# Attention with unnormalised probabilities: plain transposes, and the row sums divided out of the mixed rows

## The chip, the cores and the metric
One Trainium2 chip; the kernel runs on one of its cores. The metric is device time in microseconds (us), from the first to the last instruction and what lies around them. A measurement of this kernel can tell about 0.2% from no change.

## What is computed
An audio tower: patches become 8 x 376 tokens of 256 features; then attention, a mixture of experts, a linear recurrence and a quantised feed-forward layer, each added to its input. The change is in the attention, cut here to what matters:

```python
HEADS, DIM_HEAD = 16, 64
q = apply_rope(split_heads(x @ Wq)); k = apply_rope(split_heads(x @ Wk)); v = split_heads(x @ Wv)
sim = jnp.einsum('bid,bjd->bij', q, k) * d ** (-0.5)
sim = jnp.where(causal[None], sim, -jnp.inf)
attn = jax.nn.softmax(sim, axis=-1)
out = jnp.einsum('bij,bjd->bid', attn, v)      # batch 8, 376 tokens
return out @ Wo + bo
```

## The kernel before, in words
**Tiles.** A batch is 376 tokens in three tiles of 128, 128 and 120 rows (`TILES`, `TILE_ROWS`). The 16 heads go in 8 pairs c, as two heads of 64 features fill 128 partitions. Matrix products are made of float32r operands split into a high and a low part, three products each. Every engine has an instruction order written out by hand in `attention`, and semaphores tie the orders together. Each engine's queue is in order.

**A pair on TensorE** (`step`, L750). `turn` (L655) of the even head, `project` (L610) of q for the pair three ahead (`LEAD`), `scores` (L631) of the next pair, `turn` of the odd head, `mix` (L669) of the even head, `project` of k, `mix` of the odd head. `turn` brings the probabilities into the layout that `mix` needs: for each of the six causal blocks a matmul in f32 with a probability block as weights and a diagonal matrix of 1/row sum as the moving operand. So it transposes and normalises at once. It writes banks 4 and 5 (`BANK_PT`), columns 0 to 375. `mix` accumulates both heads of the pair in bank 6 (`BANK_O`), the even head in one half of the partitions, the odd one in the other.

**The same pair on ScalarE** (`step`, L884): `turned_high` (L841, the high part out of PSUM) of the even head, `raw_copy` (L819) of a projection, `exps` (L830) of the next pair's even head for the tile of 120 rows, `turned_high` of the odd head, the other five tiles' `exps`, `qk_split` (L824), `raw_copy`, `out_high` (L847, high part of the mixed rows), `qk_split`. In some steps `keep_turned` and `scale_rows` of the routing come in between.

**On VectorE** (`step`, L1155): `turned_low` (L1010, the low part), `swap_pairs` (L986, for the rotary embedding), `maxima` (L991) of the next pair, `turned_low` of the odd head, then `diagonals` (L1000) for both heads of the next pair: a reciprocal of the three row sums and a product of the identity with them; `swap_pairs`, and `out_low` (L1015). The maxima stand before the exponentials, since they are the bias.

**GpSimd** does the rotary products (L959, L961, L963) and the low part of q and k (L936), and scatters rows to the experts (L948).

**Between batches** (`begin`, L782): TensorE makes the values of tile 2 (L693), then the output projection of the last batch (L704, `output`), which waits for `out_low` of its last pair, then the other values.

Of the kernel before, what the change touches and what calls it, by code (L numbers as in the profile page):

```python
# [24 lines left out]
P = 128  # L25
BATCH = 8
TIME, FREQ = 750, 128
PATCH = 16
TOK = -(-TIME // PATCH) * (FREQ // PATCH)
# [3 lines left out]
HEADS, HEAD = 16, 64  # L33
# [4 lines left out]
TILES = -(-TOK // P)  # L38
TILE_ROWS = [min(P, TOK - P * i) for i in range(TILES)]
# [396 lines left out]
def attention(nc, psum, h0_rows, x_dram, weights, a, consts, ident, x_slots, h_rows, onehot, where, shared, raw_w, w_in,  # L436
              scattered, tables, made):

    ctx, sb, sem = scopes(nc, made)
    with ctx:  # L440
# [10 lines left out]
        cos = shared[:, 4 * TOK:5 * TOK]  # L451
        neg_max = sb("neg_max", [P, 2, 4])
        row_sum = sb("row_sum", [P, 2, 4])
        inv_sum = sb("inv_sum", [P, 2, 4])
        PROBS_AT = [0, P, 3 * P]
        probs = shared[:, 5 * TOK:SHARED_COLS].rearrange("p (u n) -> p u n", u=2)
        diag = sb("diag", [P, 2, TILES, P])
        pt = [sb(f"pt_{part}", [P, 2, 2, TOK], F32R) for part in ("high", "low")]
        o = [sb(f"o_{part}", [P, PAIRS, TOK], F32R) for part in ("high", "low")]
        resid = sb("resid", [P, T, DIM])  # L460
        h = sb("attn_h", [P, T, DIM])
# [33 lines left out]
        x_loaded = [sem(f"attn_x_loaded{u}") for u in range(2)]  # L495
        (resid_in, cleared, v_made, v_high, v_low, proj_made,
         raw_made, swap_made, rope_made, rot_made, qk_high, qk_ready, scores_made, max_made, exp_made,
         inv_made, diag_made, turned, pt_high, pt_ready, mixed, o_high, o_ready, out_made, out_kept) = (
            sem(n) for n in
            "resid_in cleared v_made v_high v_low proj_made "  # L500
            "raw_made swap_made rope_made rot_made qk_high qk_ready scores_made max_made exp_made "
            "inv_made diag_made turned pt_high pt_ready mixed o_high o_ready out_made out_kept".split())


        CR_RAW, CR_ROT, CR_SCORES, CR_EXP, CR_TURN, CR_PT, CR_MIX, CR_O, CR_QK = 1, 2, 4, 1, 2, 1, 2, 1, 2
# [23 lines left out]
        def probs_t(j):  # L529

            return (0, 0, TOK) if j == 0 else (1, 0, TOK - P) if j == 1 else (1, TOK - P, TOK - 2 * P)

        def padded(part, t, half):

# [26 lines left out]
        with nc.Block(no_gpsimd_drain=True) as block:  # L561
# [32 lines left out]
            def _(pe):  # L594
# [59 lines left out]

                def turn(b, h):  # L655

                    pe.wait_ge(diag_made, 16 * b + h + 1)
                    pe.wait_ge(pt_ready, 16 * b + h + CR_PT)
                    for j in range(TILES):
                        bank, col, _ = probs_t(j)  # L660
                        for it in range(j, TILES):
                            ni, nj = TILE_ROWS[it], TILE_ROWS[j]
                            at, src = col + P * (it - j), PROBS_AT[it] + P * j
                            last = pe.matmul(psum[0:nj, BANK_PT + bank, at:at + ni],  # L664
                                             probs[0:ni, h % 2, src:src + nj],
                                             diag[0:ni, h % 2, it, 0:ni], start=True, stop=True)
                    last.then_inc(turned, 1)

                def mix(b, h):  # L669

                    c, par = h // 2, h % 2
                    pe.wait_ge(pt_ready, 16 * b + h + 1 + CR_PT)
                    if par == 0:
                        pe.wait_ge(o_ready, 8 * b + c + CR_O)
                        if c == 0 and b:
                            pe.wait_ge(out_kept, T * b)
                    for j in range(TILES):
                        bank, col, n = probs_t(j)
                        nj = TILE_ROWS[j]
                        for i, (hv, hp) in enumerate(three):  # L680
                            last = pe.matmul(psum[:, BANK_O, P * j:TOK],
                                             v[hv][0:nj, j, c, HEAD * par:HEAD * par + P],
                                             pt[hp][0:nj, par, bank, col:col + n],
                                             start=(par == i == j == 0),
                                             stop=(par == 1 and i == 2 and j == TILES - 1))
                    last.then_inc(mixed, 1)

                def values(b, tiles):
                    for t in tiles:
                        for half in range(2):  # L690
                            for i, (hw, hx) in enumerate(three):
                                for c in range(2):
                                    last = pe.matmul(psum[0:TILE_ROWS[t], 2 * t + half, :],  # L693
                                                     x[:, b % 2, hx, c, P * t:P * t + TILE_ROWS[t]],
                                                     wv[hw][:, c, BANK * half:BANK * (half + 1)],
                                                     start=(i == c == 0), stop=(i == 2 and c == 1))
                            last.then_inc(v_made, 1)
# [12 lines left out]
                def turn_rows(b, c):  # L710

                    pe.wait_ge(x_made, T * (b + 1))
                    for k in range(T):
                        n = TILE_ROWS[k]
                        last = pe.transpose(turned_bank(b, c)[:, P * k:P * k + n], rows[0:n, b % 2, k, P * c:P * (c + 1)],
                                            ident[0:n, 0:n])
                    last.then_inc(x_turned, 1)
# [62 lines left out]
                def begin(b):  # L780

                    pe.wait_ge(pt_ready, 16 * b + CR_PT)  # L782
                    values(b, (2,))
                    if b:
                        pe.wait_ge(o_ready, 8 * b + CR_O)
                        output(b - 1, 0)
                        pe.wait_ge(raw_made, 16 * b + 2 * LEAD + CR_RAW)
                        output(b - 1, 1)
                        pe.wait_ge(out_kept, T * (b - 1) + 1)
                        output(b - 1, 2)  # L790
                    if b >= 2:
                        pe.wait_ge(out_kept, T * (b - 1) + 2)
                        ahead_of(b - 2)
                    pe.wait_ge(exp_made, 16 * b + 2 + CR_EXP)
                    values(b, (0, 1))
                    pe.wait_ge(v_low, 6 * b + 2)
# [9 lines left out]
                for t in range(T):  # L806
                    output(LAST, t, range(PAIRS - 1, PAIRS))
                pe.wait_ge(pt_ready, 16 * BATCH + CR_PT)
                turn_rows(LAST, 0)
                turn_rows(LAST, 1)  # L810
                logit(LAST)
# [3 lines left out]
            def _(act):  # L815
# [29 lines left out]
                                   ACT.Copy).then_inc(pt_high, 1)  # L845

                def out_high(b, c):  # L847
                    act.wait_ge(mixed, 16 * b + 2 * c + 2 + CR_MIX)
                    act.activation(o[0][:, c, :], psum[:, BANK_O, 0:TOK], ACT.Copy).then_inc(o_high, 1)

                def deviation(b):
# [124 lines left out]
            def _(dve):  # L976
# [20 lines left out]
                        if it != 0:  # L997
                            last.then_inc(max_made, 1)

                def diagonals(b, h):  # L1000

                    dve.wait_ge(exp_made, 16 * b + h + 1 + CR_EXP)
                    dve.reciprocal(inv_sum[:, h % 2, 0:TILES], row_sum[:, h % 2, 0:TILES]).then_inc(inv_made, 1)
                    dve.wait_ge(inv_made, 16 * b + h + 1)
                    dve.tensor_tensor(diag[:, h % 2, :, :],  # L1005
                                      ident[:].rearrange("p (o n) -> p o n", o=1).broadcast_to((P, TILES, P)),
                                      inv_sum[:, h % 2, 0:TILES].rearrange("p (t o) -> p t o", o=1)
                                      .broadcast_to((P, TILES, P)), ALU.mult).then_inc(diag_made, 1)

                def turned_low(b, h):  # L1010
                    dve.wait_ge(pt_high, 16 * b + h + 1)
# [143 lines left out]
                def step(b, c, more):  # L1155
                    ahead = 2 * (c + LEAD)
                    projects = more or ahead < 2 * PAIRS
                    turned_low(b, 2 * c)
                    if projects:
                        swap_pairs(b, ahead)  # L1160
                    if c + 1 < PAIRS:
                        maxima(b, c + 1)
                    elif more:
                        maxima(b + 1, 0)
                    if b and c == ROUTE_LOGITS:
                        weigh(b - 1)
                    turned_low(b, 2 * c + 1)
                    if b == LAST and c == ROUTE_PREFIX:
                        place_rows(b - 1)
                    if more or c + 1 < PAIRS:  # L1170
                        diagonals(b, 2 * c + 2)
                        diagonals(b, 2 * c + 3)
                    if projects:
                        swap_pairs(b, ahead + 1)
                    out_low(b, c)
                    if b == LAST and c == ROUTE_LOGITS + 1:
                        choose(b - 1)
                    if b == LAST and c == ROUTE_LOGITS - 1:
                        add_bo(b)
# [1 line left out]
                for n in range(2 * LEAD):  # L1181
                    swap_pairs(0, n)
                maxima(0, 0)
                diagonals(0, 0)
                diagonals(0, 1)
                for b in range(BATCH):
                    begin(b)
                    for c in range(PAIRS):
# [1152 lines left out]
```

## Time and profile before

| | us |
|---|---|
| three runs | 1788.4, 1790.22, 1790.29 (median 1790.22) |
| profiled execution | 1788.28 |
| its span, first to last instruction | 1786.5 |
| TensorE matmuls busy | 1525.2 (85% of the span) |
| VectorE busy | 1250.3 (70%) |
| ScalarE busy | 995.8 (56%) |
| GpSimd busy | 1019.2 (57%) |
| attention, 118 to 862 us: TensorE, VectorE, ScalarE, GpSimd busy | 723.0, 544.6, 473.2, 549.6 |

The profile names PE (TensorE matmul), PEld (its weight loads), DVE (VectorE), ACT (ScalarE), POOL (GpSimd). Durations of matmuls overlap, so their cost is read from the distance between starts. In each other queue too, an instruction can start a little before the one ahead of it has ended. L12 is line 12 of the kernel; tiles are named by the program's names (`expert_raw` is memory shared by the attention's raw, swapped and probability tiles). "[0.22 <-PE psum L664]" behind a row is idle time of the engine before it, and what ended it.

### The profile page before, as it was taken

How to read it: one execution, taken by the hardware profiler on the slowest of the kernel's cores; microseconds unless marked ns; L12 is line 12 of the kernel's file. 1: busy time of each engine (PE TensorE's matmuls, PEld its weight loads, DVE VectorE, ACT ScalarE, POOL GpSimd, SP SyncE). 2: the span in 40 equal slices, each digit the busy share in tenths (PEclk: the TensorE clock that was granted, in tenths of full speed). 3: DMA queues.
4: the chain of work that ended last, by engine and by line, in shares of the span. 5: the costliest groups of instructions: out<-in, count | busy, mean ns of one | idle time of the engine just before them, and what ended most of it. 6: DMA issues, size and time to landing. Idle time of an engine off the chain costs nothing. (4 is left out here: it accounts for less than half of the span.)

```text
span 1786.5 us, 31373 instructions
## 1 busy us (share of the span) xinstructions
PE 1525.2 (85%) x11301; PEld 1440.1 (81%) x11301; DVE 1250.3 (70%) x2526; ACT 995.8 (56%) x2138; POOL 1019.2 (57%) x814
## 2 busy tenths in 40 slices
PE   5389999999999999999499999999998937689129
PEld 4279999999999998998399999999987836688029
DVE  6547676868677877776346766666678569559896
ACT  4547575657575757665355555455544434459552
POOL 4479586969687777864466767766765633000000
PEclk8679999999999999999699999999999968899569
DMA  6490000000001001000465555555554331003313
GB/s 237 147 300 19 18 19 25 31 25 30 25 14 38 13 22 33 4 31 10 154 177 143 144 136 146 135 147 140 140 136 107 71 96 35 18 1 130 104 52 113
DMA packets 86129, 150.44 MB, mean 84 GB/s; under 512 B 7992, under 2 KB 63608, under 8 KB 85720
## 3 DMA queue, kind: packets, MB, share of 16 engines
q1 hardware_dynamic: 75464, 134.62, 24.6%
q0 software_dynamic: 10512, 13.83, 4.6%
q8 instruction: 90, 1.47, 0.4%
q14 instruction: 63, 0.52, 0.1%
HBM read 111.88 MB, written 49.91 MB: 91 GB/s over the span
## 5 line engine op out<-in xcount | busy, mean ns | idle before, releaser
L1534 POOL TENSOR_TENSOR expert_w_low<-expert_raw,expert_w_high 128x768 fp32r<-128x768 f32 x152 | 288.3, 1946 | 170.3 <-ACT expert_w_high L1359 164.3
L835 ACT ACTIVATE expert_raw<-psum,neg_max 120x376 f32<-120x376 f32 (+2 forms) x384 | 176.0, 479 | 99.3 <-DVE neg_max L996 99.2
L664 PE MATMUL psum<-diag,expert_raw 128*128 128x128 f32 (+2 forms) x1536 | 198.9, 279 | 8.2 <-DVE diag L1005 7.3
L1012 DVE TENSOR_TENSOR pt_low<-psum,pt_high 128x752 fp32r<-128x752 f32 x128 | 120.5, 941 | 118.1 <-ACT pt_high L844 118.1
L1506 DVE TENSOR_TENSOR expert_act_low<-expert_act,expert_act_high 128x384 fp32r<-128x384 f32 x152 | 140.1, 921 | 80.0 <-ACT expert_act_high L1397 79.4
L664 PEld LDWEIGHTS psum<-diag,expert_raw 128*128 128x128 f32 (+2 forms) x1536 | 180.3, 190 | 17.9 <-DVE diag L1005 11.2
L1397 ACT ACTIVATE expert_act_high<-expert_act 128x384 fp32r<-128x384 f32 x152 | 79.8, 525 | 204.7 <-DVE expert_act L1501 203.5
L1318 PE MATMUL psum<-slots_high,expert_w_high 128*128 128x384 f32 x608 | 160.1, 344 | 16.6 <-DVE expert_act L1501 15.4
L936 POOL TENSOR_TENSOR qk_low<-rotated,qk_high 128x376 fp32r<-128x376 f32 x128 | 144.1, 1126 | 47.1 <-ACT qk_high L828 44.3
L959 POOL TENSOR_TENSOR rotated<-expert_raw 128x376 f32<-128x376 f32 x128 | 127.9, 1000 | 56.8 <-ACT expert_raw L822 42.6
L1318 PE MATMUL psum<-slots_low,expert_w_high 128*128 128x384 f32 x608 | 156.4, 338 | 0.0
L1318 PE MATMUL psum<-slots_high,expert_w_low 128*128 128x384 f32 x608 | 156.1, 337 | 0.0
L963 POOL TENSOR_TENSOR rotated<-rotated,expert_raw 128x376 f32<-128x376 f32 x128 | 139.4, 1089 | 10.0
L1329 PE MATMUL psum<-expert_w_high,expert_act_high 128*128 128x256 f32 x456 | 135.0, 296 | 11.4 <-ACT slot_out L1379 9.9
L1359 ACT ACTIVATE expert_w_high<-expert_raw 128x768 fp32r<-128x768 f32 x152 | 126.5, 833 | 13.4 <-PEq L561 13.4
L1501 DVE TENSOR_TENSOR expert_act<-psum,silu 128x384 f32<-128x384 f32 x152 | 84.6, 556 | 67.5 <-ACT silu L1393 65.0
L1329 PE MATMUL psum<-expert_w_high,expert_act_low 128*128 128x256 f32 x456 | 129.4, 284 | 0.0
L1329 PE MATMUL psum<-expert_w_low,expert_act_high 128*128 128x256 f32 x456 | 129.3, 283 | 0.0
L961 POOL TENSOR_TENSOR expert_raw<-expert_raw,rope_sin 128x376 f32<-128x376 f32 x128 | 128.0, 1000 | 0.0
L844 ACT ACTIVATE pt_high<-psum 128x752 fp32r<-128x752 f32 x128 | 102.3, 800 | 45.1 <-PE psum L664 43.1
L1318 PEld LDWEIGHTS psum<-slots_high,expert_w_high 128*128 128x128 f32 x608 | 103.6, 192 | 23.1 <-issue 21.5
L1005 DVE TENSOR_TENSOR diag<-ident,inv_sum 128x384 f32<-128x384 f32 x128 | 116.7, 912 | 4.4
(296 smaller groups left out, 4422.6 us busy)
## 6 DMA issues: line engine op xcount, KB each, us to landing
expert_raw<-in_experts SPq DMA_DIRECT2D x152, 384.0 KB, 3.1
x_slots<-in_c_slots SPq DMA_DIRECT2D x4, 3168.0 KB, 29.4
slot_rows<-x_slots SPq DMA_DIRECT2D x19, 396.0 KB, 4.6
up_spill<-held SPq DMA_DIRECT2D x5, 1128.0 KB, 5.0
held<-up_spill SPq DMA_DIRECT2D x5, 1128.0 KB, 5.7
attn_x<-tok_xt SPq DMA_DIRECT2D x6, 752.0 KB, 4.0
x_parts<-attn_x SPq DMA_DIRECT2D x6, 752.0 KB, 4.6
patch<-in_patches SPq DMA_DIRECT2D x8, 376.0 KB, 7.0
```

What stands on the lines that cost most here:

```text
L664: last = pe.matmul(psum[0:nj, BANK_PT + bank, at:at + ni], probs[0:ni, h % 2, src:src + nj], diag[0:ni, h % 2, it, 0:ni], start=True, stop ...
L835: last = act.activation(probs[0:ni, h % 2, at:at + P * it + ni], score_bank(h % 2, it), ACT.Exp, bias=neg_max[0:ni, h % 2, it:it + 1], acc ...
L936: pool.tensor_tensor(qk[1][:, c % 2, k, :], rotated[:, k, :], qk[0][:, c % 2, k, :].bitcast(F32), ALU.subtract).then_inc(qk_ready, 1)
L959: pool.tensor_tensor(rotated[:, k, :], raw[:, k, :], cos[:], ALU.mult).then_inc(rope_made, 1)
L961: pool.tensor_tensor(swapped[:, k, :], swapped[:, k, :], sin[:], ALU.mult).then_inc(rope_made, 1)
L963: pool.tensor_tensor(rotated[:, k, :], rotated[:, k, :], swapped[:, k, :], ALU.add).then_inc(rot_made, 1)
L1012: dve.tensor_tensor(pt[1][:, h % 2, :, :], psum[:, BANK_PT:BANK_PT + 2, 0:TOK], pt[0][:, h % 2, :, :].bitcast(F32), ALU.subtract).then_inc ...
L1318: last = pe.matmul(psum[:, 2 * k + g % 2, 0:TILE_SLOTS], w[hw][:, f, at:at + P], xt[hx][:, i % 2, c, :], start=(n == c == 0), stop=(n == 2 ...
L1329: last = pe.matmul(psum[:, BANK_DOWN + s, 0:DIM], act_hl[ha][:, g % 2, P * s:P * (s + 1)], w[hw][:, f, 4 * P:4 * P + DIM], start=(n == f = ...
L1359: act.activation(w[0][:, g % RING, :], raw[:, g % RAW, :], ACT.Copy).then_inc(w_high, 1)
L1506: dve.tensor_tensor(act_hl[1][:, g % 2, :], act_f[:, g % 2, :], act_hl[0][:, g % 2, :].bitcast(F32), ALU.subtract).then_inc(low_made, 1)
L1534: pool.tensor_tensor(w[1][:, g % RING, :], raw[:, g % RAW, :], w[0][:, g % RING, :].bitcast(F32), ALU.subtract).then_inc(w_low, 1)
```

## The change
`diagonals` and the tile `diag` go. `turn` now makes plain transposes against the identity, so the probabilities stay unnormalised, and waits for the exponentials themselves. For each pair VectorE's `inverses` makes the reciprocals of both heads' row sums, each repeated over 64 columns (2 x 3 x 64 = 384 per partition). TensorE turns them with three transposes (`turn_inverse`): tiles 0 and 1 behind the odd head's turn, into columns 376 to 503 of banks 4 and 5; tile 2 ahead of the even head's mix, into bank 6. VectorE copies them to SBUF (`keep_inverse`: 256 columns, and 120 in `scale_out`) and multiplies the mixed rows in PSUM by them (`scale_out`). `out_high` waits for that product instead of for the mix.

```diff
-        inv_sum = sb("inv_sum", [P, 2, 4])
+        inv_sum = sb("inv_sum", [P, 2, TILES, P])
+        inv_rows = sb("inv_rows", [P, TOK])
-        diag = sb("diag", [P, 2, TILES, P])
...
+        def turned_inverse(it):
+            return psum[:, (BANK_PT, BANK_PT + 1, BANK_O)[it], TOK:TOK + TILE_ROWS[it]]
...
                 def turn(b, h):
-                    pe.wait_ge(diag_made, 16 * b + h + 1)
+                    pe.wait_ge(exp_made, 16 * b + h + 1 + CR_EXP)
                     pe.wait_ge(pt_ready, 16 * b + h + CR_PT)
+                    if h % 2 == 0 and 16 * b + h:
+                        pe.wait_ge(inv_kept, 2 * (8 * b + h // 2) - 1)
...
-                            last = pe.matmul(psum[0:nj, BANK_PT + bank, at:at + ni],
-                                             probs[0:ni, h % 2, src:src + nj],
-                                             diag[0:ni, h % 2, it, 0:ni], start=True, stop=True)
+                            last = pe.transpose(psum[0:nj, BANK_PT + bank, at:at + ni],
+                                                probs[0:ni, h % 2, src:src + nj], ident[0:ni, 0:ni])
+                    if h % 2:
+                        pe.wait_ge(inv_made, 8 * b + h // 2 + 1)
+                        last = turn_inverse(b, h // 2, (0, 1))
                     last.then_inc(turned, 1)
+
+                def turn_inverse(b, c, tiles):
+                    for it in tiles:
+                        ni = TILE_ROWS[it]
+                        last = pe.transpose(turned_inverse(it), inv_sum[0:ni, c % 2, it, :], ident[0:ni, 0:ni])
+                    return last
 
                 def mix(b, h):
...
                         if c == 0 and b:
                             pe.wait_ge(out_kept, T * b)
+                        turn_inverse(b, c, (2,))
...
                 def begin(b):
                     pe.wait_ge(pt_ready, 16 * b + CR_PT)
+                    if b:
+                        pe.wait_ge(inv_kept, 16 * b - 1)
                     values(b, (2,))
...
                 def out_high(b, c):
-                    act.wait_ge(mixed, 16 * b + 2 * c + 2 + CR_MIX)
+                    act.wait_ge(o_scaled, 8 * b + c + 1)
...
-                def diagonals(b, h):
-                    dve.wait_ge(exp_made, 16 * b + h + 1 + CR_EXP)
-                    dve.reciprocal(inv_sum[:, h % 2, 0:TILES], row_sum[:, h % 2, 0:TILES]).then_inc(inv_made, 1)
-                    dve.wait_ge(inv_made, 16 * b + h + 1)
-                    dve.tensor_tensor(diag[:, h % 2, :, :],
-                                      ident[:].rearrange("p (o n) -> p o n", o=1).broadcast_to((P, TILES, P)),
-                                      inv_sum[:, h % 2, 0:TILES].rearrange("p (t o) -> p t o", o=1)
-                                      .broadcast_to((P, TILES, P)), ALU.mult).then_inc(diag_made, 1)
+                def inverses(b, c):
+                    dve.wait_ge(exp_made, 16 * b + 2 * c + 2 + CR_EXP)
+                    dve.reciprocal(inv_sum[:, c % 2, :, :].rearrange("p t (u n) -> p u t n", u=2),
+                                   row_sum[:, :, 0:TILES].rearrange("p u (t o) -> p u t o", o=1)
+                                   .broadcast_to((P, 2, TILES, HEAD))).then_inc(inv_made, 1)
+
+                def keep_inverse(b, c):
+                    dve.tensor_copy(inv_rows[:, 0:2 * P].rearrange("p (t n) -> p t n", t=2),
+                                    psum[:, BANK_PT:BANK_PT + 2, TOK:TOK + P]).then_inc(inv_kept, 1)
+
+                def scale_out(b, c):
+                    dve.wait_ge(mixed, 16 * b + 2 * c + 2 + CR_MIX)
+                    dve.tensor_copy(inv_rows[:, 2 * P:TOK], turned_inverse(2)).then_inc(inv_kept, 1)
+                    dve.wait_ge(inv_kept, 2 * (8 * b + c + 1))
+                    dve.tensor_tensor(psum[:, BANK_O, 0:TOK], psum[:, BANK_O, 0:TOK], inv_rows[:], ALU.mult).then_inc(o_scaled, 1)
...
                     turned_low(b, 2 * c + 1)
+                    keep_inverse(b, c)
...
                     if more or c + 1 < PAIRS:
-                        diagonals(b, 2 * c + 2)
-                        diagonals(b, 2 * c + 3)
+                        inverses(b, c + 1)
                     if projects:
                         swap_pairs(b, ahead + 1)
+                    scale_out(b, c)
                     out_low(b, c)
```

## Rows read from the trace of the kernel before

**Rows 1.** The page: granted TensorE clock by slice; one group of GpSimd.
```profile
PEclk8679999999999999999699999999999968899569
...
L936 POOL TENSOR_TENSOR qk_low<-rotated,qk_high 128x376 fp32r<-128x376 f32 x128 | 144.1, 1126 | 47.1 <-ACT qk_high L828 44.3
```
**Rows 2.** Timeline of TensorE, one pair of batch 0: start, us, what, records.
```profile
145.82 1.54 PE L664 MATMUL psum<-diag,expert_raw 128*128 128x128 f32 x12
147.12 0.93 PE L626 MATMUL psum<-x_parts,L_attn_Wq_high 128*128 128x376 f32 x4
...
154.81 1.54 PE L664 MATMUL psum<-diag,expert_raw 128*128 128x128 f32 x12
```
**Rows 3.** Timeline of TensorE: three transposes of the routing, then a turn.
```profile
239.45 0.55 PE L715 MATMUL psum<-ident,x_rows 128*128 128x128 f32 x3
239.83 0.61 PE L664 MATMUL psum<-diag,expert_raw 128*128 128x128 f32 x4
```
**Rows 4.** Timeline of ScalarE in the pair of rows 2.
```profile
147.39 0.80 ACT L844 ACTIVATE pt_high<-psum 128x752 fp32r<-128x752 f32 x1 [0.22 <-PE psum L664]
...
150.59 0.57 ACT L835 ACTIVATE expert_raw<-psum,neg_max 120x376 f32<-120x376 f32 x1 [1.68 <-DVE neg_max L996]
...
151.64 0.80 ACT L844 ACTIVATE pt_high<-psum 128x752 fp32r<-128x752 f32 x1 [0.38 <-PE psum L664]
152.33 0.36 ACT L835 ACTIVATE expert_raw<-psum,neg_max 128x128 f32<-128x128 f32 x1
...
154.87 0.51 ACT L822 ACTIVATE expert_raw<-psum 128x376 f32<-128x376 f32 x1
155.23 0.52 ACT L849 ACTIVATE o_high<-psum 128x376 fp32r<-128x376 f32 x1
```
**Rows 5.** Timeline of VectorE in the same pair.
```profile
149.58 1.84 DVE L996 TENSOR_REDUCE neg_max<-psum 120x2 f32<-120x752 f32 x3
...
154.63 0.18 DVE L1003 RECIPROCAL inv_sum<-row_sum 128x3 f32<-128x3 f32 x1 [0.55 <-ACT expert_raw L835]
154.84 0.56 DVE L1005 TENSOR_TENSOR diag<-ident,inv_sum 128x384 f32<-128x384 f32 x1
...
155.43 0.59 DVE L989 STREAM_SHUFFLE expert_raw<-expert_raw 128x376 f32<-128x376 f32 x1
...
155.90 0.54 DVE L1017 TENSOR_TENSOR o_low<-psum,o_high 128x376 fp32r<-128x376 f32 x1
```
**Rows 6.** Single lines of VectorE: count, ns (min/median/max), first and last start, shape.
```profile
L2098 DVE RECIPROCAL q_steps<-q_steps x5: 163/164/164, 1541.5 to 1726.6; 128x1 f32<-128x1 f32 x5
...
L1003 DVE RECIPROCAL inv_sum<-row_sum x128: 159/165/177, 111.8 to 834.8; 128x3 f32<-128x3 f32 x128
...
L1456 DVE RECIPROCAL q_inv<-q_scale x12: 227/228/229, 952.7 to 1262.8; 128x12 f32<-128x12 f32 x12
...
L1083 DVE TENSOR_TENSOR odds_gt<-odds_gt,odds_eq x8: 207/207/210, 291.7 to 861.2; 128x48 f32<-128x48 f32 x8
```
**Rows 7.** Timeline of TensorE: first turns of batches 3 and 4, and what lies between.
```profile
393.28 0.38 PE L664 MATMUL psum<-diag,expert_raw 128*128 128x128 f32 x2
...
469.88 1.14 PE L693 MATMUL psum<-L_attn_Wv_high,x_parts 128*120 128x512 f32 x4
...
472.70 0.52 PE L704 MATMUL psum<-L_attn_Wo_high,o_high 128*128 128x256 f32 x3
...
487.20 1.48 PE L664 MATMUL psum<-diag,expert_raw 128*128 128x128 f32 x12
```
**Rows 8.** ScalarE at a batch's first exponentials (timeline); its scale_rows (line 862).
```profile
491.91 1.28 ACT L835 ACT_TABLE_LOAD   x1 [1.67 <-DVE neg_max L996]
...
L862 ACT ACTIVATE x_rows<-attn_h,row_shift,row_rstd x24: 585/590/650, 218.6 to 854.2; 128x256 f32<-128x256 f32 x16, 120x256 f32<-120x256 f32 x8
```
**Rows 9.** Experts: TensorE's timeline; windows (PE, PEld, DVE, ACT, POOL busy, clock, DMA).
```profile
1309.22 0.43 PE L1329 MATMUL psum<-expert_w_high,expert_act_high 128*128 128x256 f32 x1 [1.89 <-ACT slot_out L1379]
...
1309.40:1312.80 3.40, 3.40 (x15) 3.40 (x16) 2.03 (x11) 2.13 (x4) 1.86 (x2) 0.50 0.21 80
1312.80:1316.00 3.20, 3.20 (x23) 3.20 (x22) 2.89 (x6) 0.70 (x2) 3.05 (x2) 1.00 0.56 144
```

More of the change, by code:

```diff
@@ L497, in attention @@
          raw_made, swap_made, rope_made, rot_made, qk_high, qk_ready, scores_made, max_made, exp_made,
-         inv_made, diag_made, turned, pt_high, pt_ready, mixed, o_high, o_ready, out_made, out_kept) = (
+         inv_made, inv_kept, o_scaled, turned, pt_high, pt_ready, mixed, o_high, o_ready, out_made, out_kept) = (
             sem(n) for n in
@@ L501, in attention @@
             "raw_made swap_made rope_made rot_made qk_high qk_ready scores_made max_made exp_made "
-            "inv_made diag_made turned pt_high pt_ready mixed o_high o_ready out_made out_kept".split())
+            "inv_made inv_kept o_scaled turned pt_high pt_ready mixed o_high o_ready out_made out_kept".split())
         CR_RAW, CR_ROT, CR_SCORES, CR_EXP, CR_TURN, CR_PT, CR_MIX, CR_O, CR_QK = 1, 2, 4, 1, 2, 1, 2, 1, 2
@@ L808, in _ @@
                 pe.wait_ge(pt_ready, 16 * BATCH + CR_PT)
+                pe.wait_ge(inv_kept, 16 * BATCH - 1)
                 turn_rows(LAST, 0)
@@ L1183, in _ @@
                 maxima(0, 0)
-                diagonals(0, 0)
-                diagonals(0, 1)
+                inverses(0, 0)
                 for b in range(BATCH):
```

## The prediction
> **What bounds the kernel now.** I read the page first, then the timeline of one head pair on TensorE, then the same stretch on ScalarE and VectorE. The page shows the clock granted in full (nines) through the attention, slices 3 to 19, and GpSimd's rotary work in operations of at most 1.13 us [rows 1]. In batch 0 one pair takes 154.81 - 145.82 = 8.99 us of TensorE, with no idle time marked: the turn of the even head starts at 145.82, that of the next pair at 154.81 [rows 2]. So TensorE sets the pace there. ScalarE has waits of 0.22, 1.68 and 0.38 us in that pair [rows 4] and VectorE one of 0.55 [rows 5]: they have slack of about 1 us a pair, no more. In batch 3 the turns of successive batches lie 487.20 - 393.28 = 93.92 us apart; from 469.88 on, 17.32 of it are values and output projection, which leaves 76.6 for eight pairs, 9.57 each [rows 7].
>
> **TensorE, what the change takes away.** A turn is six f32 matmuls in twelve records, and twelve starts take 147.12 - 145.82 = 1.30 us [rows 2]. A transpose of the same 128x128 f32 tiles is one record each, and three starts take 239.83 - 239.45 = 0.38 us at the same clock [rows 3]. They follow a short wait; in a row I take the 0.11 us pitch of one record of the turn (1.30/12). Six transposes are then 0.65, so a head saves 0.65 and a pair 1.30. Added are three transposes of the inverse, 0.33. TensorE falls from 8.99 to about 8.0 us a pair, 64 x 0.99 = 63 us in all, if TensorE stays the bound.
>
> **VectorE, what is swapped.** Per pair go two reciprocals of 3 elements (0.18) and two diagonals (0.56) [rows 5], 1.5 us. Four operations come: one reciprocal of 2x3x64 = 384 elements per partition; a copy of 256 columns out of PSUM; a copy of 120; a multiplication over 376 columns, PSUM and SBUF into PSUM. The last resembles o_low, 0.54 [rows 5]. From 154.84's 384 columns in 0.56 and 48 columns in 0.207 a one-pass element costs (558-207)/336 = 1.04 ns [rows 5, 6], so the copies are 0.54 - 120 x 1.04 ns = 0.41 and 0.54 - 256 x 1.04 ns = 0.27.
>
> **The reciprocal is the term that decides.** Three lengths of it are in the trace: 1 element 164 ns, 3 elements 159 to 177, 12 elements 228 [rows 6]. Between 1 and 12 an element costs 64/11 = 5.8 ns, over five times the one-pass price; between the slowest 3 and 12 it is 51/9 = 5.7, between the fastest 3 and 12 69/9 = 7.7. For 384 elements that is 164 + 383 x 5.8 ns = 2.4 us, and 3.1 us with 7.7. The low bound is the one-pass operation of that length, the diagonal's 0.56 [rows 5]. Between ends this far apart I take 2.4: it rests on the same operation, with nearly the same start-up in all three rows.
>
> **Where these lie.** Before, ScalarE took the mixed rows (out_high) as soon as they were mixed. Now out_high waits for o_scaled, the last of VectorE's new work, which stands in its queue behind turned_low, keep_inverse, inverses and swap_pairs; inverses itself waits for both exponentials of the next pair. Behind out_high in ScalarE's queue stand qk_split and the next pair's turned_high, on which everything of the next pair rests. That closes a ring. From one turned_high of an even head (147.39, zero) to the next:
> exponentials of the 120-row tile start at 150.59, +3.20; VectorE comes to the maxima at 149.58 with no idle time, so a faster TensorE doesn't shorten it [rows 4, 5]. That exponential 0.57, then turned_high of the odd head, 152.33 - 151.64 = 0.69; its 0.38 wait goes, as TensorE is ahead. Five tile exponentials, until VectorE sees them: 154.63 - 152.33 = 2.30. Reciprocal 2.40. swap_pairs 155.90 - 155.43 = 0.47. Copy 0.27 and its semaphore 0.03. Multiplication 0.54, to ScalarE 0.04. out_high and qk_split, 376-column copies whose starts lie 155.23 - 154.87 = 0.36 apart, 0.72. Sum 11.23 us [rows 4, 5].
> TensorE needs 8.0 of it and idles 3.2: the next odd turn waits for turned_low of the even head, which now comes late. keep_inverse costs nothing: it lies in the 0.4 us and more in which VectorE waits for the exponentials anyhow (with that cover gone 0.41 a pair). GpSimd's eight operations, at most 9.0 us [rows 1], and one scatter of about an operation's length (estimate) fit below 11.2; with that cover gone a pair would take some 10. The new waits of turn on inv_kept, and of values on it, are behind keep_inverse, which ends before the odd mix: nothing.
>
> **A whole batch.** First turn to its turned_high: 0.65, and 147.39 - 147.12 = 0.27 from the end of the turn [rows 2, 4]: 0.9. Seven rings, 78.6. Work of ScalarE that was hidden under TensorE and now lengthens the ring: a table load 1.28, three scale_rows at 0.59 [rows 8], two keep_turned at 0.36: 3.8. In the last pair out_high starts 10.5 us in (11.23 less 0.72), o_low ends 0.56 + 0.54 later, and only then may the output projection start: 11.6. Values of tile 2 cover 2.82 us of that after the last mix [rows 7], so TensorE stands about 2 us. From the start of the output projection to the next turn 487.20 - 472.70 = 14.5 as before. Sum 109.4 against 93.9: +15.5 a batch. Seven batches +108; the last one has pairs without projections and no next batch, say +14. Batch 0 pairs were at 8.99 and lose more a pair, but have none of the 3.8: about the same.
> **Clock.** Each ring now has one stretch of about 2.5 us without a matmul. Before 1309.22 TensorE stood 1.89 us, and the granted clock was 0.50, the 1.2 GHz level, for the next 3.4 us, then 1.00, the 2.4 GHz level [rows 9]. A fall of that length costs TensorE 1.7 us a pair, of which the 3.2 idle hide nearly all; for the beginnings of batches and the turn of the odd head I add 7 us (estimate).
> Sum on the profiled execution: 1788.3 + 108 + 14 + 7 = 1917. The median of the runs, 1790.2, lies 1.9 higher: **1919 us**.
>
> **Rivals.**
> *Eight passes per element.* If a long reciprocal costs eight one-pass elements of 1.04 ns, 8.3 each, it takes 3.3 us, the ring grows by 0.9, and 63 rings add 57, 1976. Against it stands the line of 5.8 [rows 6]; for it, that no reciprocal here is longer than 12. 12%.
> The Trainium skill, "VectorE: DVE Perf Modes", section "First, the fixed hardware budget", says that the reciprocal is an iterative divide with a repeat count of 8. By that rule the time would be this rival's 1976; the trace agrees that an element costs many passes, not that it is eight.
> *Cheap reciprocal.* If the slope is a start-up effect and 384 elements take about the diagonal's 0.56, the ring goes by ScalarE instead: the qk_split and raw copy that follow the exponentials end 0.36 + 0.51 after them, less the 0.17 by which VectorE sees them late, so 0.7 stands in place of 2.4: ring 9.5, 63 x 1.7 = 107 less: 1812. Still slower, as o_scaled holds ScalarE. 6%.
> *TensorE stays the bound*, the case on the other side. Place: ScalarE's out_high. Price: 63 us off, and some 8 of waits on the diagonals: 1719. It decides only if the ring is below 9.0, that is if reciprocal, copy and multiplication together are 1.0 instead of 3.2, or VectorE and ScalarE overlap more than their order allows. For it speaks only that TensorE is the bound now [rows 2]. 3%.
> *The clock stays at the lower level.* TensorE's 8.0 become 16 a pair, 4.8 over the ring, 64 times, and the 17.3 of each beginning double: 1919 + 307 + 138, about 2360. Against it: after 1.89 us of idle time the fall lasted 3.4 us and the next stretch was full again [rows 9]. 4%.
> The Trainium skill, "TensorE: Matmul & The Clock Gate", section "Part 4: PE-mode transpose", says that transposes don't bring the full clock as matmuls do. Here the three transposes at 239.45 ran at the pitch of the full clock between matmuls [rows 3], and no stretch here is made of transposes alone. By the rule the sum would move towards this rival.
> *The transposes take two records after all*, so that TensorE is relieved of nothing: it would need 8.99 + 0.66 = 9.7 of 11.2 us, and the time stays.
>
> **Numbers.** The ring with the long reciprocal gets 75%. Its own range is 1885 to 1955: 0.5 us of ring either way (63 x 0.5 = 32), from the estimates of the copy, the multiplication and the hand-overs. The range 1880 to 1975 takes in most of the eight-pass case; outside stay cheap reciprocal, TensorE-bound and low clock, 13%, and some of the rest. A measurement can tell 0.2%, 3.6 us. Faster only by the TensorE case: 3%; same 1%; slower 96%.
>
> **What would show it.** Right: the RECIPROCAL in inverses at 2.3 to 2.5 us; turn at 0.65 to 0.7 us from start to next; ScalarE idle before o_high for 2 to 3 us with VectorE's psum multiplication as releaser; pairs 11.0 to 11.5 apart from batch 1 on; TensorE idle before the odd turn, waiting for pt_low; halves of the clock in short pieces. Wrong: a reciprocal under 1 us, TensorE without idle time, pairs near 8 us, or o_high waiting for something else.

## The result, and the profile after

The changed kernel takes 1932.3 us (median of four runs, 1930.4 to 1933.4) against 1789.4 before: 1.080 times the time, 95% interval 1.078 to 1.082. Forecast were 1919 us and a range of 1880 to 1975.

The page of the changed kernel; the second group of numbers is busy time, its share of the span, and instructions, then come the clock by slice and the groups that matter (busy us, mean ns, idle time of the engine before, and the releaser: what ended most of that idle time).
```profile
span 1929.5 us, 30236 instructions
...
PE 1525.6 (79%) x10725; PEld 1424.5 (74%) x10725; DVE 1345.9 (70%) x2526; ACT 984.7 (51%) x2138; POOL 988.9 (51%) x814
...
PEclk8688989999898999999978999999999987799659
...
L955 POOL TENSOR_TENSOR qk_low<-rotated,qk_high 128x376 fp32r<-128x376 f32 x128 | 126.5, 988 | 168.2 <-ACT qk_high L847 168.2
L1022 DVE RECIPROCAL inv_sum<-row_sum 128x384 f32<-128x384 f32 x64 | 163.4, 2553 | 59.4 <-ACT expert_raw L854 59.4
...
L670 PE MATMUL psum<-ident,expert_raw 128*128 128x128 f32 (+2 forms) x768 | 120.9, 299 | 88.6 <-DVE pt_low L1040 88.0
...
L868 ACT ACTIVATE o_high<-psum 128x376 fp32r<-128x376 f32 x64 | 31.0, 484 | 196.6 <-DVE psum L1036 196.6
```
Three new things stand here. A reciprocal takes 2.55 us and there are 64. ScalarE's o_high (line 868, out_high) stands 196.6 us in all, released by VectorE's product in PSUM (line 1036), where before ScalarE stood 4.4 us in all ahead of it. And TensorE, whose turns (line 670) have half as many records (768 for 1536), waits 88 us for pt_low. GpSimd's qk_low fell from 1126 ns [rows 1] to 988: in the kernel before, the 61 of its 128 that ran beside a product of diagonals and o_low took 1.23 us in the mean and the 48 beside the maxima 0.98, and the products of diagonals are gone. But qk_low is not what a pair waits for.

One pair of batch 0, ScalarE's timeline (start, us, what, idle time before and releaser):
```profile
153.52 0.79 ACT L863 ACTIVATE pt_high<-psum 128x752 fp32r<-128x752 f32 x1
...
156.70 0.57 ACT L854 ACTIVATE expert_raw<-psum,neg_max 120x376 f32<-120x376 f32 x1 [2.02 <-DVE neg_max L1015]
...
157.36 0.80 ACT L863 ACTIVATE pt_high<-psum 128x752 fp32r<-128x752 f32 x1
158.06 0.36 ACT L854 ACTIVATE expert_raw<-psum,neg_max 128x128 f32<-128x128 f32 x1
...
164.20 0.48 ACT L868 ACTIVATE o_high<-psum 128x376 fp32r<-128x376 f32 x1 [3.10 <-DVE psum L1036]
164.58 0.51 ACT L847 ACTIVATE qk_high<-rotated 128x376 fp32r<-128x376 f32 x1
164.99 0.79 ACT L863 ACTIVATE pt_high<-psum 128x752 fp32r<-128x752 f32 x1
```
and VectorE's:
```profile
155.69 1.85 DVE L1015 TENSOR_REDUCE neg_max<-psum 120x2 f32<-120x752 f32 x3
...
159.05 0.41 DVE L1028 COPY inv_rows<-psum 128x256 f32<-128x256 f32 x1
160.35 2.55 DVE L1022 RECIPROCAL inv_sum<-row_sum 128x384 f32<-128x384 f32 x1 [0.89 <-ACT expert_raw L854]
...
162.84 0.57 DVE L1008 STREAM_SHUFFLE expert_raw<-expert_raw 128x376 f32<-128x376 f32 x1
...
163.31 0.26 DVE L1034 COPY inv_rows<-psum 128x120 f32<-128x120 f32 x1
163.61 0.56 DVE L1036 TENSOR_TENSOR psum<-psum,inv_rows 128x376 f32<-128x376 f32 x1
```
Read them as one ring: maxima to exponential (156.70), turned_high of the odd head (157.36), five exponentials, reciprocal (160.35), swap_pairs (162.84), copy (163.31), product (163.61), out_high (164.20), qk_split, and the next turned_high at 164.99, 11.47 us after the last one; the pair before it took 11.37. Before it was 8.99 us from turn to turn [rows 2]. keep_inverse (159.05) lies in VectorE's wait for the exponentials, which is still 0.89 us long behind it.

TensorE in the same pair:
```profile
155.43 1.47 PE L670 MATMUL psum<-ident,expert_raw 128*128 128x128 f32 x6 [1.86 <-DVE pt_low L1040]
156.69 0.83 PE L681 MATMUL psum<-ident,inv_sum 128*128 128x128 f32 x3
...
161.36 0.83 PE L670 MATMUL psum<-ident,expert_raw 128*128 128x128 f32 x6
161.95 0.94 PE L630 MATMUL psum<-x_parts,L_attn_Wq_high 128*128 128x376 f32 x4
```
The turn at 161.36 takes 0.59 us to the next start, where it took 1.30 [rows 2]. The one at 155.43 takes 1.26: it follows 1.86 us of idle time, and its granted clock is 0.50 (the 1.2 GHz level) where that of the turn at 161.36 is 1.00 (2.4 GHz). It costs the ring 0.1 us: turned_high starts 0.66 us behind the exponential here (156.70 to 157.36), and 0.57 in the pair before (145.33 to 145.90), whose odd turn ran at the full clock. That is the difference between 11.47 and 11.37.

Over six batches the first turned_high of a batch comes (894.36 - 225.92)/6 = 111.4 us after the last batch's, against the 93.9 of [rows 7].

### The profile page after: what moved, and what is told of

Its sections match the earlier page's. It is cut to its first block and busy times, and to the rows that moved or that the text cites. A ratio compares the mean times of both kernels' runs of the same rounds, so it can differ in the third digit from the quotient of the medians.

```text
span 1929.5 us, 30236 instructions
## 1 busy us (share of the span) xinstructions
PE 1525.6 (79%) x10725; PEld 1424.5 (74%) x10725; DVE 1345.9 (70%) x2526; ACT 984.7 (51%) x2138; POOL 988.9 (51%) x814
## 5 line engine op out<-in xcount | busy, mean ns | idle before, releaser
L955 POOL TENSOR_TENSOR qk_low<-rotated,qk_high 128x376 fp32r<-128x376 f32 x128 | 126.5, 988 | 168.2 <-ACT qk_high L847 168.2
L1022 DVE RECIPROCAL inv_sum<-row_sum 128x384 f32<-128x384 f32 x64 | 163.4, 2553 | 59.4 <-ACT expert_raw L854 59.4
L670 PE MATMUL psum<-ident,expert_raw 128*128 128x128 f32 (+2 forms) x768 | 120.9, 299 | 88.6 <-DVE pt_low L1040 88.0
L670 PEld LDWEIGHTS psum<-ident,expert_raw 128*128 128x128 f32 (+2 forms) x768 | 93.1, 155 | 99.8 <-ACT expert_raw L841 69.2
L1357 PE MATMUL psum<-expert_w_high,expert_act_high 128*128 128x256 f32 x456 | 134.3, 295 | 11.5 <-ACT slot_out L1407 10.1
L697 PE MATMUL psum<-pt_high,v_high 128*128 128x376 f32 (+2 forms) x384 | 128.3, 334 | 12.4 <-DVE pt_low L1040 12.3
L868 ACT ACTIVATE o_high<-psum 128x376 fp32r<-128x376 f32 x64 | 31.0, 484 | 196.6 <-DVE psum L1036 196.6
L982 POOL TENSOR_TENSOR rotated<-rotated,expert_raw 128x376 f32<-128x376 f32 x128 | 126.1, 985 | 10.0
```

What stands on the lines that cost most here:

```text
L670: last = pe.transpose(psum[0:nj, BANK_PT + bank, at:at + ni], probs[0:ni, h % 2, src:src + nj], ident[0:ni, 0:ni])
L697: last = pe.matmul(psum[:, BANK_O, P * j:TOK], v[hv][0:nj, j, c, HEAD * par:HEAD * par + P], pt[hp][0:nj, par, bank, col:col + n], start=( ...
L955: pool.tensor_tensor(qk[1][:, c % 2, k, :], rotated[:, k, :], qk[0][:, c % 2, k, :].bitcast(F32), ALU.subtract).then_inc(qk_ready, 1)
L1022: dve.reciprocal(inv_sum[:, c % 2, :, :].rearrange("p t (u n) -> p u t n", u=2), row_sum[:, :, 0:TILES].rearrange("p u (t o) -> p u t o", o=1)
L1357: last = pe.matmul(psum[:, BANK_DOWN + s, 0:DIM], act_hl[ha][:, g % 2, P * s:P * (s + 1)], w[hw][:, f, 4 * P:4 * P + DIM], start=(n == f = ...
```

## The experiments

All are edits of the changed kernel, but for the reciprocals, which were put into the kernel before. Its time in these runs was 1788.6.

### 1. A short reciprocal, spread by a copy

```diff
-                    dve.reciprocal(inv_sum[:, c % 2, :, :].rearrange("p t (u n) -> p u t n", u=2),
-                                   row_sum[:, :, 0:TILES]... .broadcast_to((P, 2, TILES, HEAD))).then_inc(inv_made, 1)
+                    link(dve.reciprocal(inv_few[:], row_sum[:, :, 0:TILES]))
+                    dve.tensor_copy(inv_sum[:, c % 2, :, :].rearrange("p t (u n) -> p u t n", u=2),
+                                    inv_few[:]... .broadcast_to((P, 2, TILES, HEAD))).then_inc(inv_made, 1)
```


> The reciprocal of each pair is made of the 6 row sums only and then spread over the 384 columns by a copy. Ring theory (a pair lasts as long as the way exponentials, reciprocal, swap_pairs, scale_out, out_high, qk_split, turned_high): reciprocal 0.2 and copy 0.6 us stand for 2.55, the raw copy then hides them, a pair takes 9.6 us for 11.37, 63 x 1.75 = 110 us less: 1822. Rival (the new waits between VectorE and ScalarE and the lower clock cost the time, whatever the reciprocal's length): above 1900.

Measured: 1820.2 us, 1.0175 times the kernel before (1.0158 to 1.0192). 112 us of the 143 are the reciprocal's length. VectorE in a pair of batch 3, and the raw copy of ScalarE:
```profile
456.64 0.19 DVE L1023 RECIPROCAL inv_few<-row_sum 128x6 f32<-128x6 f32 x1 [0.89 <-ACT expert_raw L855]
456.87 0.36 DVE L1024 COPY inv_sum<-inv_few 128x384 f32<-128x384 f32 x1
457.44 0.01 DVE L1009 LOAD_MASK_SELECT expert_raw<-expert_raw  x1 [0.21 <-issue]
...
458.22 0.56 DVE L1038 TENSOR_TENSOR psum<-psum,inv_rows 128x376 f32<-128x376 f32 x1
...
456.86 0.53 ACT L842 ACTIVATE expert_raw<-psum 128x376 f32<-128x376 f32 x1
```
0.19 and 0.36 us stand for 2.55, and ahead of swap_pairs (457.44) VectorE now stands 0.21 us until ScalarE's raw copy, which ends at 457.39, is there: that bounds what this edit alone can give. Pairs of batch 0 take 9.70 us, still more than 8.99.

### 2. The turn by matmuls again

```diff
-                            last = pe.transpose(psum[0:nj, BANK_PT + bank, at:at + ni],
-                                                probs[0:ni, h % 2, src:src + nj], ident[0:ni, 0:ni])
+                            last = pe.matmul(psum[0:nj, BANK_PT + bank, at:at + ni],
+                                             probs[0:ni, h % 2, src:src + nj], ident[0:ni, 0:ni], start=True, stop=True)
```


> The six transposes of a turn are matmuls against the identity again (two records each), all else as after the change. Ring theory: TensorE has 3.2 us of idle time in a pair and takes 1.3 of it; 1932 to 1945, and the clock dips get fewer. Rival (TensorE's length or its clock still sets the pair): 63 x 1.3 = 82 us more, 2014.

Measured: 1965.0 us (1961.5 to 1970.6), 33 us more than with transposes: more than the at most 13 of the expectation, less than half of TensorE's added work. On the profiled executions 23 us of it lie between the pairs of the batches and 5 in the beginnings of batches, which have a turn on their way (27.8 to 28.1 us for 26.7 to 27.3). The trace tells the two kinds of pair apart. The second, third and fourth pair of batch 2, one stretch each (length, busy time of PE, PEld, DVE, ACT, POOL, granted clock, DMA):
```profile
358.70:370.50 11.80, 9.36 (x87) 8.94 (x87) 8.80 (x16) 6.67 (x21) 8.74 (x10) 1.00 0.03 11
370.50:383.70 13.20, 10.98 (x87) 10.56 (x87) 8.81 (x16) 6.88 (x21) 8.79 (x10) 0.87 0.03 12
383.70:395.90 12.20, 10.84 (x82) 10.39 (x84) 8.47 (x16) 6.70 (x21) 8.26 (x10) 0.86 0.04 12
```
Where the clock is 1.00 a pair takes what it took with transposes (11.38, 11.75 or 11.86, by its place in the batch). Where it falls for 3.4 us (0.87 over the pair; 6.8 us in three pairs) it takes 11.8 to 14.2. Of the 56 distances between pairs within a batch 25 have a fall in them, and each is longer than its like without one (the pair with the router's logits has one in every batch, and so has the last distance of batch 7, which is a kind by itself: they have no such like). Of the 31 without a fall only the very first is long, 12.1. So within a batch the 1.3 us hide at the full clock, as forecast, and at the lower level they don't. In the changed kernel itself 29 of the 56 have a fall (133 us at the lower level within the attention), but the transposes leave enough slack: they lengthen a pair by 0.1 us at most, but for the one with the router's logits, which takes 11.5 to 13.3. The trace shows why, in batch 4 (a pair of 12.89) and in batch 6 (11.47):
```profile
510.10 2.49 PE L741 MATMUL psum<-router_w,router_x 128*128 128x4 f32 x12 [1.55 <-ACT expert_raw L841]
512.45 1.48 PE L670 MATMUL psum<-ident,expert_raw 128*128 128x128 f32 x6
...
514.39 0.80 ACT L863 ACTIVATE pt_high<-psum 128x752 fp32r<-128x752 f32 x1 [1.66 <-PE psum L681]
...
845.49 1.48 PE L741 MATMUL psum<-router_w,router_x 128*128 128x4 f32 x12 [1.52 <-ACT expert_raw L841]
846.83 0.84 PE L670 MATMUL psum<-ident,expert_raw 128*128 128x128 f32 x6
```
The logits (line 741) stand ahead of the odd turn in TensorE's queue. At the full clock (batch 6) logits and turn take 1.34 + 0.68 us and are just in time for ScalarE. At a granted clock of 0.55 and 0.50 (batch 4) they take 2.35 + 1.27, and ScalarE waits 1.66 us for the odd turn.

### 3. Without the scaling

```diff
-                    act.wait_ge(o_scaled, 8 * b + c + 1)
+                    act.wait_ge(mixed, 16 * b + 2 * c + 2 + CR_MIX)
...
-                    dve.tensor_copy(inv_rows[:, 2 * P:TOK], turned_inverse(2)).then_inc(inv_kept, 1)
-                    dve.wait_ge(inv_kept, 2 * (8 * b + c + 1))
-                    dve.tensor_tensor(psum[:, BANK_O, 0:TOK], psum[:, BANK_O, 0:TOK], inv_rows[:], ALU.mult).then_inc(o_scaled, 1)
+                    dve.tensor_copy(inv_rows[:, 2 * P:TOK], inv_sum[:, c % 2, 2, 0:TOK - 2 * P]).then_inc(inv_kept, 1)
```


> Leaves the division by the row sums out: out_high waits for the mix as before the change, the multiplication is gone, the copy of 120 columns reads SBUF; reciprocal, inverse transposes and the other copy stay. Ring theory: ScalarE is no longer held by VectorE, but VectorE's own queue is: exponentials seen at 6.74, reciprocal to 9.2, swap to 9.7, copy and out_low to 10.4, and only then the next turned_low, so 9.6 us a pair and 1820 in all. Rival (the reciprocal costs only through o_scaled): TensorE or GpSimd bounds again, 8.2 to 9.0 us a pair, 1730 to 1780. Rival (hand-overs don't matter): 1932.

Measured: 1800.0 us in one run. VectorE in one pair:
```profile
145.52 2.55 DVE L1022 RECIPROCAL inv_sum<-row_sum 128x384 f32<-128x384 f32 x1 [0.89 <-ACT expert_raw L854]
...
148.60 0.55 DVE L1043 TENSOR_TENSOR o_low<-psum,o_high 128x376 fp32r<-128x376 f32 x1
149.06 0.93 DVE L1038 TENSOR_TENSOR pt_low<-psum,pt_high 128x752 fp32r<-128x752 f32 x1
...
150.40 1.85 DVE L1015 TENSOR_REDUCE neg_max<-psum 120x2 f32<-120x752 f32 x3
152.81 0.94 DVE L1038 TENSOR_TENSOR pt_low<-psum,pt_high 128x752 fp32r<-128x752 f32 x1 [0.55 <-ACT pt_high L863]
...
154.97 2.55 DVE L1022 RECIPROCAL inv_sum<-row_sum 128x384 f32<-128x384 f32 x1 [0.89 <-ACT expert_raw L854]
```
From reciprocal to reciprocal 9.45 us, and from 145.52 to the maxima not a gap: pt_low follows o_low at once. ScalarE is free and waits for VectorE's maxima instead. The mechanism is that of the expectation; 9.45 came where 9.6 was put down, and the pairs with routing, at 9.3 to 9.9, lose less than they did in the ring over ScalarE, hence 1800 and not 1820. The reciprocal costs even where nobody waits for its result (the trace shows no wait of any engine for it here): it fills the queue.

### 4. Scaling first

```diff
+                    scale_out(b, c)
                     if more or c + 1 < PAIRS:
                         inverses(b, c + 1)
                     if projects:
                         swap_pairs(b, ahead + 1)
-                    scale_out(b, c)
```


> Only the order on VectorE changes: scale_out stands before inverses and swap_pairs, so ScalarE gets its mixed rows at 7.9 us of the pair and not at 10.5. Ring theory: now VectorE's queue closes the ring: scale 7.0 to 7.9, reciprocal to 10.3, swap to 10.75, out_low to 11.2, then turned_low, 10.4 us a pair, 62 less: 1870. Rival (ScalarE's wait was the whole of the loss): 8.9 us a pair, 1775. Rival (the reciprocal's length alone counts, wherever it stands): 1932.

Measured: 1867.1 us in one run, pairs of 10.37. VectorE:
```profile
158.49 0.28 DVE L1034 COPY inv_rows<-psum 128x120 f32<-128x120 f32 x1 [1.17 <-PE psum L697]
158.81 0.56 DVE L1036 TENSOR_TENSOR psum<-psum,inv_rows 128x376 f32<-128x376 f32 x1
159.27 2.54 DVE L1022 RECIPROCAL inv_sum<-row_sum 128x384 f32<-128x384 f32 x1
...
162.21 0.53 DVE L1045 TENSOR_TENSOR o_low<-psum,o_high 128x376 fp32r<-128x376 f32 x1
162.66 0.93 DVE L1040 TENSOR_TENSOR pt_low<-psum,pt_high 128x752 fp32r<-128x752 f32 x1
```
The same operations in another order are 65 us cheaper. The wait that is left is VectorE's queue from the end of the mix (158.49) to pt_low (162.66), without a gap.

### 5. Both, and the output later still

short_and_first is 1 and 4 together. late_out puts, on top of it, out_high and out_low of a pair behind the next even head's turned_high and turned_low (in a batch's last pair they stay):
```diff
                     turned_high(b, 2 * c)
+                    if c:
+                        out_high(b, c - 1)
...
-                    out_high(b, c)
+                    if c == PAIRS - 1:
+                        out_high(b, c)
```
and so for out_low.

> Both edits that helped, together: reciprocal of 6 row sums spread by a copy (0.2 and 0.36 us), and scale_out ahead of inverses and swap_pairs. Ring theory: ScalarE has its mixed rows at 7.85 us of the pair, out_high and qk_split bring the next turned_high to 8.7; VectorE's queue ends at 9.3, just in time. 8.7 us a pair where nothing else holds it, but GpSimd's operations and scatters need 9.3 in four pairs of a batch: from 1820 down 63 x 1.0 and up 8, about 1765, faster than the kernel before. If the two gains overlap (the shorter of the two waits is left): 1800 to 1820.

> As short_and_first, and out_high and out_low of a pair are put off until after the next even head's turned_high and turned_low (not in a batch's last pair). Ring theory: scale_out leaves the ring altogether, VectorE's out_low comes ahead of the maxima instead: 3.65 + 0.55 + 0.69 + 2.13 + 0.41 + 0.36 + 0.41 = 8.2 us, at which GpSimd bounds, so 1750 to 1760. If GpSimd sets the pair in short_and_first already: the same as that one within 5 us.

Measured: short_and_first 1765.7 us, 0.9873 times the kernel before (0.9856 to 0.9889); late_out 1761.7 us, 0.9848 (0.9832 to 0.9864). VectorE of short_and_first in one pair:
```profile
162.29 0.28 DVE L1036 COPY inv_rows<-psum 128x120 f32<-128x120 f32 x1 [1.18 <-PE psum L698]
162.61 0.56 DVE L1038 TENSOR_TENSOR psum<-psum,inv_rows 128x376 f32<-128x376 f32 x1
163.07 0.18 DVE L1023 RECIPROCAL inv_few<-row_sum 128x6 f32<-128x6 f32 x1
163.29 0.38 DVE L1024 COPY inv_sum<-inv_few 128x384 f32<-128x384 f32 x1
```
Pairs of batch 0 take 8.72, those of later batches 8.7 to 9.5 (the first of a batch 10.5; the last batch has one of 10.1 and one of 7.8). The two gains nearly add up: 112 and 65 us by themselves, 167 together. late_out's pairs of batch 0 fall to 8.43, but in the batches with scatters five of seven stay at 8.8 to 9.3, and its beginnings of batches are 0.7 us longer (25.66 against 24.96 to 25.01): 4 us in all, with intervals that overlap, where the first reading of the expectation gave 6 to 16. It is the second reading of the expectation (GpSimd sets the pair, the same within 5 us), and the trace fits it: over the second and third pair of batch 3, 18.4 us, GpSimd goes from one operation to the next, nine to a pair, the scatter among them, and never stands longer than 0.15 us, while VectorE and ScalarE stand 1.9 to 2.5 us in each pair. No edit relieved GpSimd, so this is read and not shown by a run.

### 6. The transposes, where the ring is out of the way

Edit 2 on top of short_and_first.

> short_and_first with the six transposes of a turn made by matmuls against the identity again. Ring theory: with the ring down to 8.7 us TensorE is near the bound, and its 1.3 us a pair come back: 8.0 + 1.3 = 9.3 us a pair, and 9.6 where the routing's transposes come in: 0.6 in each of 63 pairs, 1766 + 38 = about 1800. Then the plain transposes are worth what was counted for them, once the ring is out of the way. Rival (TensorE has slack here still, the gain over the kernel before comes from VectorE and GpSimd being relieved of the diagonals): 1766 to 1775.

Measured: 1799.7 us, 1.0060 (1.0043 to 1.0077). Pairs of batch 0 take 9.28 to 9.33 (the first 9.62), and TensorE is busy for the whole of them: here it is the bound. So the plain transposes are worth 34 us once the ring is short. It also shows that the rest of the change (row sums divided out by VectorE) is no gain by itself: with matmuls for the turns, the rest in this order is 0.6% slower than the kernel before.

### 7. The reciprocal by itself

```diff
+                apart(dve.memset(flat, 2.0))
+                for n in (24, 96, 384, 752):
+                    apart(dve.reciprocal(rout[:, 0:n], flat[:, 0:n]))
+                    apart(dve.tensor_copy(rout[:, 0:n], flat[:, 0:n]))
+                apart(dve.reciprocal(rout[:, 0:384]..., flat[:, 0:6]... .broadcast_to((P, 2, TILES, HEAD))))
```


> The kernel before, with reciprocals and copies of 24, 96, 384 and 752 columns of SBUF ahead of the attention's VectorE work, each apart, and one reciprocal of 6 values each read 64 times. Straight line of 6.2 ns an element (164 ns for 1, 2553 for 384): 0.31, 0.76, 2.55 and 4.85 us, the spread one 2.55 too. Eight passes of 1.04 ns (8.3 ns): the long ones above 3.2 and 6.4. If the spread reading is what made it slow: the plain 384 below 1 us.

VectorE's timeline:
```profile
88.58 0.30 DVE L998 RECIPROCAL router_x<-attn_h 128x24 f32<-128x24 f32 x1
...
89.12 0.75 DVE L998 RECIPROCAL router_x<-attn_h 128x96 f32<-128x96 f32 x1
...
90.16 2.55 DVE L998 RECIPROCAL router_x<-attn_h 128x384 f32<-128x384 f32 x1
92.75 0.36 DVE L999 COPY router_x<-attn_h 128x384 f32<-128x384 f32 x1
93.14 4.85 DVE L998 RECIPROCAL router_x<-attn_h 128x752 f32<-128x752 f32 x1
98.03 0.55 DVE L999 COPY router_x<-attn_h 128x752 f32<-128x752 f32 x1
98.62 2.55 DVE L1000 RECIPROCAL router_x<-attn_h 128x384 f32<-128x384 f32 x1
```
A straight line, (4854 - 2553)/368 = 6.25 ns an element, and the reading of each value 64 times costs nothing.

## Why the prediction was right, step by step

**TensorE, what the change takes away**: right. Forecast 0.65 us a turn, measured 0.59, and experiment 6 gives 34 us for it where without it TensorE bounds, against 38 expected.

**The reciprocal is the term that decides**: right, and under-sized. 2.55 us came for 2.4. The line through 1 and 12 elements was too flat, since the shortest operations don't lie on the line of the long ones: 153 + 6.25 ns for each element meets 12, 24, 96, 384 and 752 elements, but gives 159 for one and 172 for 3, where 164 and 165 (median) stand [rows 6]. "Eight passes per element" was wrong in size: 6.25 ns are six times the one-pass 1.04, and 8.3 would have made 3.3 us. So the count of 8 in the Trainium skill, "VectorE: DVE Perf Modes", section "First, the fixed hardware budget", read as eight one-pass elements, doesn't give the measured time.

**Where these lie**: the ring was right, link by link; forecast 11.23, measured 11.37 to 11.47 in batch 0. From start to start, reciprocal to swap_pairs is 2.49 for 2.40 (swap_pairs starts a little before the reciprocal ends, as it did before), out_high and qk_split are 0.79 for 0.72, and the other links agree within 0.02, but for the 0.1 of the slow turn. So the ring is 0.14 longer, and 63 x 0.14 = 9 us of the 13 by which the time was missed. Experiments 1 and 4 each change one of its parts and land within 3 us of what the ring gives (1822 and 1870 expected); together they land at 1765.7 for 1765. The rival "cheap reciprocal", forecast at 1812, is close to what experiment 1 is, 1820. "TensorE stays the bound" asked for a ring under 9.0: in short_and_first it is 8.7, and the kernel is faster than before, though not by that rival's 63 us, as the ring is still longer than the 8.0 put down for TensorE. One reading of the prediction was incomplete: with the waits of 0.77 and 1.04 us ahead of pt_low VectorE stood 2.4 us in the pair of [rows 5], not 0.55, and ScalarE 2.5, so their slack was more than "about 1 us". No term of the sum rests on it.

**keep_inverse costs nothing, GpSimd fits**: shown by the 0.89 us of wait left behind the copy, and by GpSimd's 168 us of waits for qk_high.

**A whole batch**: forecast +15.5 us, measured 111.4 - 93.9 = 17.5. Of the 2.0 between them 1.0 is the longer ring (7 x 0.14), and 1.0 is the pair of the router's logits, 12.4 us in the mean of batches 1 to 6 for 11.4. Nothing was put down for that pair in the batch; its excess is the clock's (experiment 2) and belongs to the term below. The pairs 11.0 to 11.5 apart, which the prediction named as a sign, are the exception from batch 1 on: five of seven carry the work of the prediction's own 3.8 us, and take 11.7 to 13.2.

**The sum**: on the profiled executions 143 us came for the 129 put down. From the first turned_high of batch 0 to that of batch 7 it was 125, for 108 and the clock's 7; 7 of these 10 us are the longer ring (49 x 0.14), and 2 are there because batch 1 of the kernel before took 91.7 us and not the 93.9 of batch 3. The last batch and what follows took 19 for the 14 that the prediction only guessed ("say"). Only the start came lower, by 1. So the errors are small, and as nearly all are on one side, it isn't by cancelling that the total is close.

**Clock**: right in kind and in size. The falls last 3.4 us, in some places 6.8, come in 29 of 56 pairs and not in each, and hide under the ring but for the logits' pair. Seven such pairs take 6.6 us more than 11.38 each, which is what became of the 7 us put down; they do lie at the odd turn, but in one pair of a batch, and the beginnings of batches came at the 27 us of the forecast. That the size fits is luck, as the logits were not in the estimate. Experiment 2 shows what the falls cost where TensorE has 1.3 us less slack: most of the 23 us between pairs, where its expectation had at most 13 in all. That was a miss: the sum looked at TensorE's slack at the full clock alone. The Trainium skill, "TensorE: Matmul & The Clock Gate", section "Part 4: PE-mode transpose", has it that transposes don't bring the full clock. No fall here needs that rule: ahead of each of the 34 in the attention TensorE had stood for 1.5 to 3.5 us, the six transposes at 161.36 ran at the full clock, and the kernel of experiment 2, without transposes of the probabilities, shows the falls too.

## What to carry to other kernels

Before an operation is moved from one engine to another, write down the ring that the new wait closes, with the queues that stand behind it, and sum it; busy shares (VectorE 70% before and after) showed nothing of it. A reciprocal is paid by the element, so it is made of the few values that differ and spread by a copy: 0.55 us for 2.55. And the order within one queue can be worth as much as the work: what another engine waits for goes ahead of what nobody waits for yet.

## What was not expected of the hardware

A copy between SBUF tiles in f32 takes 0.36 us for 384 columns and 0.55 for 752, about 0.5 ns a column, where a tensor_tensor of 384 takes 0.56 [rows 5]. The length of one pause doesn't tell whether the clock falls: here it fell to the lower level in the 1.86 us of idle time before 155.43, while it stayed in full after the 2.72 us ahead of the turn at 132.68.
